# Score stacks of an attention kernel: built by a bounce through DRAM, or by twelve on-chip copies a step

## The reference

```python
qkv = x @ w_qkv + b_qkv                       # layer 0
scores = einsum('bhtd,bhsd->bhts', q, k) / sqrt(8) + rpe_bias
out = einsum('bhts,bhsd->bhtd', softmax(scores), v) @ w_out + b_out
...
scores = where(causal, q @ k.T / sqrt(8), neg)  # layer 1
new_attn = resid_gain * softmax(scores) + skip_gain * eye - centre_gain * uniform
out = (new_attn @ v) @ cproj_w
```

## Time and profile before

| | |
|---|---|
| timed runs | 1042.18, 1039.54, 1040.69 us (median 1040.69) |
| span of the profiled execution | 1042.1 us; the page gives nothing around it |
| busy | PE 83%, PEld 53%, DVE 70%, ACT 44%, POOL 38% |
| chain that ended last | PE 19%, issue 14%, POOL 8%, DMA 5% |
| DMA queue of SPq | 96780 packets, 76.54 MB, 32.4% of 16 engines |
| HBM | 45.69 MB read, 41.11 MB written |
| one step of layer 0, layer 1 | about 22.7 us, 17.55 us |

### The profile page before, as it was taken

How to read it: one execution, slowest core, us unless ns; L and a number is a source line. 1 busy time by engine, 2 the same in 40 slices (tenths; PEclk the granted TensorE clock), 3 DMA queues, 4 the chain that set the end, 5 groups by cost and what they waited for, 6 DMA issues and landing times.

```text
span 1042.1 us, 22685 instructions
## 1 busy us (share of the span) xinstructions
PE 867.5 (83%) x7795; PEld 551.3 (53%) x7814; DVE 728.4 (70%) x1177; ACT 456.1 (44%) x808; POOL 393.3 (38%) x421
## 2 busy tenths in 40 slices
PE   1884887999999999987999998525689999999986
PEld 0742443555555555544555555314467667676763
DVE  5564686999899999985665555365456767676763
ACT  1251333545444554533433333258354445454532
POOL 7007772111111111100577776673134334344432
PEclk9996788999999999997999999856899999999998
DMA  4797441332223333204122122240544453435320
GB/s 135 232 142 173 111 113 44 82 75 62 62 63 74 76 81 72 61 7 140 37 59 53 54 56 56 69 125 16 118 98 89 98 103 97 103 97 103 97 44 11
DMA packets 105527, 88.21 MB, mean 85 GB/s; under 512 B 12565, under 2 KB 97497, under 8 KB 102409
## 3 DMA queue, kind: packets, MB, share of 16 engines
q1 hardware_dynamic: 96780, 76.54, 32.4%
q0 software_dynamic: 4352, 8.99, 2.8%
q10 hardware_dynamic: 4352, 2.10, 0.9%
HBM read 45.69 MB, written 41.11 MB: 83 GB/s over the span
## 4 chain that ended last, share of the span: by engine, by line
PE 19%; issue 14%; POOL 8%; DMA 5%; ACT 3%; DVE 3%; SPq 1%; POOLq 0%; ACTq 0%; DVEq 0%
PE ps L666 7%; POOL probs L1137 5%; PE ps L687 3%; DMA ks<-parts_d 3%; PE ps L678 2%; PE ps L660 2%; POOL qkr L1124 1%; ACT rows L888 1%; PE ps L668 1%; POOL qk L1129 1%; DMA parts_d<-qk 1%; PE ps L1469 1%; DVE mx L1191 1%; PE ps L1411 1%; DMA probs<-mixed 0%
## 5 line engine op out<-in xcount | busy, mean ns | idle before, releaser
L1191 DVE TENSOR_REDUCE mx<-ps 128x4 f32<-128x1024 f32 (+1 forms) x224 | 269.5, 1217 | 106.2 <-PE ps L1411 68.4
L1338 ACT ACTIVATE probs<-probs 128x1024 f32<-128x1024 f32 x128 | 135.3, 1057 | 165.6 <-DVE probs L1201 163.1
L1201 DVE TENSOR_TENSOR probs<-ps,tabB 128x1024 f32<-128x1024 f32 x128 | 152.4, 1212 | 3.6 <-PE ps L1431 3.6
L1343 ACT ACTIVATE probs<-ps 128x1024 f32<-128x1024 f32 x96 | 96.5, 1024 | 96.3 <-PE ps L1469 38.6
L1460 PE MATMUL ps<-probs,vpad 128*32 128x256 f32 (+1 forms) x2048 | 132.5, 365 | 3.0 <-ACT probs L1338 1.1
L1137 POOL TENSOR_TENSOR probs<-probs 128x512 f32<-128x512 f32 x64 | 78.9, 1264 | 136.7 <-PE ps L1460 136.7
L1403 PE MATMUL ps<-tabA,eyeb 128*128 128x512 bf16 x256 | 101.9, 398 | 31.2 <-DVE probs L1201 18.0
L1405 PE MATMUL ps<-ks,qs 96*128 96x256 bf16 x512 | 101.7, 281 | 0.0
L1431 PE MATMUL ps<-qs,ks 99*128 99x256 bf16 x512 | 76.7, 279 | 11.1 <-DVE mx L1191 6.0
L666 PE MATMUL ps<-qs,probs 128*128 x144 | 81.7, 650 | 1.4
L1460 PE MATMUL ps<-probs,onespad 128*32 128x256 f32 x1024 | 82.3, 394 | 0.0
(11 more groups left out here) (227 smaller groups left out, 1593.1 us busy)
## 6 DMA issues: line engine op xcount, KB each, us to landing
parts_d<-qk SPq DMA_DIRECT2D x64, 192.0 KB, 2.3
qs<-parts_d SPq DMA_DIRECT2D x32, 384.0 KB, 4.9
ks<-parts_d SPq DMA_DIRECT2D x32, 384.0 KB, 6.7
parts_d<-qk SPq DMA_DIRECT2D x64, 128.0 KB, 1.9
slots_in<-probs SPq DMA_DIRECT2D x1, 4680.0 KB
probs<-slots_in SPq DMA_DIRECT2D x72, 65.0 KB, 1.8
parts_d<-qk SPq DMA_DIRECT2D x64, 64.0 KB, 1.6
probs<-mixed SPq DMA_DIRECT2D x16, 256.0 KB, 3.3
```

The source lines that it names most:

```text
L1191: nc.vector.tensor_reduce(mx[:, s.buf(), t, heads[0]:heads[-1] + 1], ring[:, slot].rearrange("p (h n) -> p h n", n=w), AX.X, ALU.max).then ...
L1201: nc.vector.tensor_tensor(probs[:, j, :].rearrange("p (h n) -> p h n", n=T), ring[:, slot].rearrange("p (h n) -> p h n", n=T), v.tabB[:, h ...
L1338: nc.scalar.activation(probs[:, j, :], probs[:, j, :], ACT.Exp).then_inc(exp_done, 1)
L1343: nc.scalar.activation(probs[:, j, :], ring[:, slot], ACT.Exp).then_inc(exp_done, 1)
```

## The change

The DRAM tensor `parts_d`, the six stores and the two loads go. When a part is made, SPq issues one DMA for each group of 8 stack partitions that it fills, straight from the 128 partitions of `qk3` to the 8 of `qs` or `ks`: six for part 0, four for part 1, two for part 2. All twelve count on `stack_ld`. The wait for the buffer's former use comes ahead of the first of them, where it stood ahead of the loads. ACT's line 1310 waits for the twelve copies of the former batch where it waited for the six stores.

```diff
-PART_DMAS = 6
+STACK_DMAS = 12
...
-        v.parts_d = nc.dram_tensor("parts_d", (3, 2, PAIRS, P, T), BF16, kind="Internal")
...
             def stacks(s):
 
                 b = s.buf(1)
-                first, second, third, stored, scored = ahead(
-                    s.n(1) + 1, s.n(1) + 1, s.n(1) + 1, 16 * PART_DMAS * (s.turn(1) + 1), NU * (s.n(-2) + 1))
+                first, second, third, scored = ahead(s.n(1) + 1, s.n(1) + 1, s.n(1) + 1, NU * (s.n(-2) + 1))
+                if s.has(-2):
+                    sp.wait_ge(full["B"], scored)
                 for c, made, wait in ((0, s1_done, first), (1, s2_done, second), (2, s3_done, third)):
                     sp.wait_ge(made, wait)
-                    for a in range(2):
-                        rows = PART_ROWS[a][c]
-                        sp.dma_start(v.parts_d[b, a, rows].rearrange("r p t -> p r t"),
-                                     qk3[:, a, c, :].unsqueeze(1).broadcast_to([P, PARTS - c, T])
-                                     ).then_inc(part_st[b], 16)
-                sp.wait_ge(part_st[b], stored)
-                if s.has(-2):
-                    sp.wait_ge(full["B"], scored)
-                for a, stack in ((0, qs), (1, ks)):
-                    sp.dma_start(stack[0:QROWS, b].rearrange("r h t -> r (h t)"),
-                                 v.parts_d[b, a].rearrange("r (d h) t -> (r d) (h t)", d=HD)).then_inc(stack_ld[b], 16)
+                    for a, stack in ((0, qs), (1, ks)):
+                        part = qk3[:, a, c, :]
+                        for r in range(PAIRS)[PART_ROWS[a][c]]:
+                            sp.dma_start(stack[r * HD:r * HD + HD, b], part).then_inc(stack_ld[b], 16)
...
                 if s.has():
-                    act.wait_ge(part_st[s.buf()], 16 * PART_DMAS * (s.turn() + 1))
+                    act.wait_ge(stack_ld[s.buf()], 16 * STACK_DMAS * (s.turn() + 1))
                 nc.scalar.activation(qk3[:, :, 0, :], qkf[:], ACT.Copy).then_inc(s1_done, 1)
```

More of the change, by code:

```diff
@@ L1015, in attention @@
     rd_done, on_done = sem("rd"), sem("on")
-    part_st = [sem(f"part_st{i}") for i in range(3)]
     stack_ld = [sem(f"stack_ld{i}") for i in range(3)]
@@ L1025, in attention @@
         out_st = [sem(f"out_st{i}") for i in range(3)]
-    STACK_DMAS = 2
     first = Step(-1, 0, 3, B)
```

## The result

The changed kernel takes 1068.97 us (median of four runs, 1065.56 to 1072.68), beside 1041.43 us for the kernel before in the same session. The ratio is 1.026, 95% interval 1.021 to 1.031: slower, where faster was forecast. The profiled execution has a span of 1070.5 us and a time of 1072.7 us; granted clock 0.928 in the mean.

What follows compares the result with a forecast made beforehand. PE's waits on the stacks, at most about 30 us, were taken as the bound; 9.0 steady + 4.6 start of layer 1 + 0 layer 0 = 13.6 us off the profiled 1042.1: 1028.5, or 1027 in runs; range 1019 to 1036, 8 in 10 1018 to 1069.

Steps and rivals of the forecast that it cites:

- What bounds it: PE's waits on the stacks: 17.5 us in layer 1, 12.4 us starting layer 0; at most about 30 us to gain.
- The thresholds: Stacks landing within 13.4 us of part 0 give all the gain, at 14.3 us none, later they cost.
- Price of a copy: One 8 KB row per engine taken at 0.80 us from the loads; twelve land 11.0 us after part 0.
- the same formula: Landing of the stacks after part 0 is 1.6 us plus twelve times a copy's price, used for the threshold of 1.06 us.
- The bound above: Highest row price, from the maxima's DMA landing: 1.15 to 1.35 us, twelve landing 15.4 to 17.6 us after part 0.
- Steady steps: Layer 1, batches 3 to 15: waits on the stacks go, 9.0 us gained.
- The slow rival: Copies queue at two ports, 1.15 us each, landing 15.4 us after part 0: 28 us lost, 1069 us; chance 0.30.
- Start of layer 1: First batches of layer 1: 2.1 us gained at batch 1 and 2.5 at batch 2, together 4.6 us.
- Layer 0: Steady steps hide the copies; the start put at zero, with 3.6 us gained or 4.4 us lost as bounds.
- Issuing: Twelve DMAs on SPq at 0.43 to 0.76 us each, 5.2 to 9.1 us, covered by idle time.
- Engines: Each copy taken to use eight engines, each with 16 packets and one row of 8 KB.
- HBM traffic: Named as a sign of being right: HBM traffic lower by 25 MB each way.

Runs made afterwards that it cites:

- e1: Changed kernel with each copy's eight rows 12 partitions apart instead of side by side, same twelve copies; 1024.47 us, ratio 0.979.
- e7: Changed kernel with ten copies instead of twelve, first group of part 0 left out for q and k, rows neighbouring; 1038.05 us, ratio 0.995.
- e4: Kernel before, bounce through DRAM kept, with its two loads writing every second partition (0 to 94) instead of 0 to 47; 1029.0 us, ratio 0.983.
- e5: Changed kernel with a copy's rows 2 partitions apart, two groups interleaved, two rows in each of four blocks of four; 1021.85 us, one run.
- e12: Changed kernel with every copy moved four rows down, still filling two aligned blocks of four; 1074.54 us, ratio 1.027.
- e13: Changed kernel with row groups 4 and 5 at partitions 64 to 79 instead of 32 to 47, order of copies kept; 1060.48 us, ratio 1.014.
- e14: Changed kernel with q and k copies in turn, and row groups 4 and 5 at partitions 64 to 79; 1068.29 us, ratio 1.020.
- e9: Changed kernel with every copy moved two rows down, filling one aligned block of four and half of each block beside it; 1037.13 us, one run.
- e3: Changed kernel with the twelve copies in another order, q and k in turn, rows unchanged; 1085.9 us, ratio 1.039.
- e2: Changed kernel with each copy's eight rows 6 partitions apart, all within the stacks' 48 partitions; 1026.6 us, ratio 0.980.
- e6: Changed kernel with each copy's eight rows 8 partitions apart, one row in each of eight blocks; 1021.95 us, one run.
- e8: Changed kernel with rows 12 apart and K's copies issued by ScalarE in layer 0's first two steps and layer 1's first; 1024.71 us, ratio 0.984.
- e11: Changed kernel with rows 8 partitions apart and K's copies of the first steps in both layers issued by ScalarE; 1026.63 us, ratio 0.984.

## Why the prediction was wrong

1. *What bounds it*: right. The thresholds, 13.4 us for all of the gain and 14.3 for none, hold: e1's queue is empty at 9.2 us and it takes PE's own step (16.79 us against 16.80 read), e7 lands at 13.8 and 14.2 us in steps that just begin to wait, the changed kernel lands at 15.7 us and loses.
2. *Price of a copy*: this is the step that failed. "I take 0.80 us, since size, destination and partitions are the same." Measured, 1.17 us by the same formula, over the 1.06 from which the change loses. The destination was the same, but the loads wrote 48 partitions at once and a copy writes eight, in two blocks of four; only e4 showed that the 0.80 us were themselves a crowded price. The bound above, from the maxima (1.15 us), three rows of one block, was the nearer row, and it was passed over because its packets ran at 56 GB/s, 0.44 us a row. Packets of a DMA that runs alone did not show the price: the first copy of a step has 31 ns a packet too, the middle ones 89.
3. *Steady steps*: by that one price the sign turned, from -9.0 to +16.5 us. The slow rival's sum was 17, its step 18.85 us against 18.93 measured, its time 1069 against 1068.97. That the time agrees so closely is luck: the rival had 17, 6.7 and 4.4 us for steady steps, start of layer 1 and layer 0, where 16.5, 5.9, 4.9 and 1.0 at the end were measured, and the errors cancel. The steps at a granted clock of 0.91 were in neither sum, and the waits covered them.
4. *Start of layer 1*: "Two of the four microseconds are taken back by the edit at line 1310" named the right chain with too small a size. ACT waits 3.73 us there for batch 0's copies, unit 0 of batch 0 comes 3.9 us later than before instead of 4.0 sooner, and batch 1 ends 10.1 us late (5.2 of them lost here) beside the rival's 4.7. In e1, landing early, unit 0 of batch 1 comes at 743.03, 6.4 us sooner than before, of which 3.0 are gained at this start (its middle part begins at 689.60, 3.4 us sooner).
5. *Layer 0*: the steady steps hide it, as said. The start doesn't: the first stack is 2.7 us late (94.50 against 91.81), ACT's held part 0 makes that 3.8 at batch 1, and 4.9 reach the middle part. The forecast had put zero, with 4.4 lost as the bound, just short of what was lost.
6. *Issuing*: 0.613 us an instruction, 0.655 apart, within 0.43 to 0.76, and hidden in the changed kernel. With spread rows it is what sets the landing.
7. *Engines*: eight were taken. The bursts of e1, where no copy runs into the next, reach 5 tenths of 16 engines and no more in slices of 0.25 us, which fits eight with a packet each. The 62% of 802:806 is ten packets at a time, more than eight engines could hold one by one, so either an engine has more than one packet on its way or copies overlap on other engines; no run here tells which. The Trainium skill ("DMA: Bandwidth & Descriptors", Why a DMA increments its semaphore by 16 and not by 1) gives eight, which e1's bursts agree with and the 62% neither proves nor refutes.
8. *HBM traffic*: lower by the 25 MB each way that were named, and no gain came with it: the changed kernel is slower, and e4, which moves all the bytes of the bounce, is faster by 1.7%.

What the rival got right is size and mechanism: copies that follow one another into the same few partitions are slow. The same rule stands in the Trainium skill ("SBUF — State Buffer", Door 1: The DMA port swizzle): a port serves four neighbouring partitions and the four that lie 32 further on, and takes 27 GB/s. The runs agree on the block of four (e5, e12); e13 and e14 fit the partner 32 on without proving it. A copy of 64 KB over two ports is by the page an estimated 1.2 us; 1.17 was measured. What the page does not give is e9: its four middle rows fill a block as before, yet the copies run at 92 GB/s. Nor does it give the first copy of a step, whose packets are as quick with neighbouring rows (31 ns) as with spread ones (30 ns).

*Open*: why one full block beside two half-filled ones is so much cheaper than two full ones (the source side, whose sixteen partitions a row are neighbours too, was not varied); why e9's steps differ among themselves; why the crowding shows only from about the third copy on; and what in the order of the copies makes e3 slow, of which the move by 32 rows took little out of the waits.

## What to carry to other kernels

Before replacing a DMA by one to few partitions, look at which partitions it writes: spread its rows so that at most two fall into an aligned block of four, which costs one stride in the destination and decided here between +2.6% and -2.1%. Take the price of such a DMA from the landing of the one that crowds the same few partitions, even if it is a smaller transfer, and not from a large one that is spread over more, nor from the packets of one that runs alone. And ask whether the duration you borrow is itself a crowded one: the plain kernel had 1.7% waiting in the stride of its two loads.

## What the runs showed of the hardware that was not expected

- 512 B packets from SBUF to eight partitions, over three steps (781:831): 28 ns with at most two rows in a block of four (e1, e2, e5, e6), 41 ns with one full block and two halves (e9), 72 ns with two full ones (after, e12). Within a step of the kernel after it is 31 ns for the first copy and 89 in the middle (804:812).
- Loads from HBM feel it too: 6.60 us to 4.65 for the same 768 KB when they go to every second partition (e4), though their descriptors are 8 KB long.
- SPq needs 0.61 us to issue one copy of 128 packets to eight partitions, with neighbouring or spread rows, beside 0.43 us for a store.
- With no wait left in the steady steps, the start of layer 1 keeps 2.0 us and that of layer 0 9.7 (e1); a second issuing queue took 2.8 us off the 9.7 in e8, but only 0.4 off the 9.3 of the other placement (e11 against e6), and neither moved the time.
